# Rebuilding the first attention of a four-layer program: keys, queries and values through DRAM, transposed once, the diagonal masked on PE

## The reference, cut to what matters

```python
def _L1_xattn_ref(q, latent_kv, Wq, Wkv_expand, Wout):
    ...
    qp = q @ Wq.T
    kv = latent_kv @ Wkv_expand.T
    k, v = jnp.split(kv, 2, axis=-1)
    ...
    scores = jnp.einsum('bhqd,bhkd->bhqk', qh, kh) * inv_sqrt_d
    scores = jnp.where(causal, scores, jnp.finfo(scores.dtype).min)
    attn = jax.nn.softmax(scores, axis=-1)
    out = jnp.einsum('bhqk,bhkd->bhqd', attn, vh)
    ...
    return out @ Wout.T
```

## Time and profile before

| | us |
|---|---|
| median of 3 runs | 3899.13 (3897.04 to 3908.89) |
| the profiled execution | 3866.58 |
| its span | 3865.0 |
| busy: PE, DVE, ACT, POOL | 3227.9, 2331.7, 1878.8, 608.3 |
| mean granted clock of PE | 0.912 |

### The profile page before, as it was taken

One profiled execution on the slowest core, in us unless ns is written; L12 is line 12 of the kernel. 1 busy time (PEld: TensorE's weight loads), 2 busy tenths in 40 slices (PEclk: granted clock), 3 DMA queues, 4 the chain that ended last, 5 costly groups with the idle time before them and its releaser, 6 DMA issues. The chain is left out here.

```text
span 3865.0 us, 62264 instructions
## 1 busy us (share of the span) xinstructions
PE 3227.9 (84%) x16914; PEld 2254.7 (58%) x16918; DVE 2331.7 (60%) x3995; ACT 1878.8 (49%) x3267; POOL 608.3 (16%) x901
## 2 busy tenths in 40 slices
PE   4339996899985399956999789899899589979998
PEld 2127775666663288843333367788777333337886
DVE  6964445455535233347899545566556798965565
ACT  5643333255532155534777633466533477773343
POOL 2420000444420300021000130122111000010000
PEclk7669998999997599976999899999999699989999
DMA  4324444220001333334222252476644322212223
GB/s 145 137 99 137 138 138 130 104 82 0 0 12 54 111 109 103 109 114 153 53 52 53 80 184 93 154 245 238 209 137 128 119 53 52 57 31 80 95 94 115
DMA packets 191373, 405.52 MB, mean 105 GB/s; under 512 B 45893, under 2 KB 46021, under 8 KB 190579
## 3 DMA queue, kind: packets, MB, share of 16 engines
q1 hardware_dynamic: 157906, 287.52, 24.1%
q0 software_dynamic: 22480, 96.23, 7.3%
q10 hardware_dynamic: 10864, 20.45, 1.4%
HBM read 313.37 MB, written 88.08 MB: 104 GB/s over the span
## 5 line engine op out<-in xcount | busy, mean ns | idle before, releaser
L1646 DVE TENSOR_REDUCE at_maxima<-psum 128x1 f32<-128x512 f32 (+1 forms) x768 | 614.0, 861 | 53.8 <-PE psum L1547 52.0
L1625 ACT ACTIVATE at_probs<-psum 128x512 f32<-128x512 f32 x1024 | 528.8, 604 | 234.1 <-PE psum L1563 233.7
L1563 PE MATMUL psum<-at_qT,at_kT 50*128 50x512 f32 x1024 | 385.8, 458 | 90.4 <-ACT at_probs L1625 49.2
L573 PE MATMUL psum<-f_xT_hi,ffn_w_hi 128*128 x1024 | 407.8, 398 | 9.7 <-DVE f_xT_lo L313 2.2
L573 PE MATMUL psum<-f_xT_lo,ffn_w_hi 128*128 x1024 | 406.9, 397 | 0.0
L1563 PEld LDWEIGHTS psum<-at_qT,at_kT 50*128 50x128 f32 x1024 | 174.6, 191 | 385.2 <-ACT at_probs L1625 282.4
L1547 PE MATMUL psum<-at_kT,at_qT 48*128 48x512 f32 x1024 | 388.1, 481 | 9.6 <-DVE at_maxima L1646 7.7
L1576 PE MATMUL psum<-at_probs,at_vals 128*32 128x512 f32 x2048 | 282.4, 623 | 0.0
L590 PE MATMUL psum<-ffn_w_hi,ffn_hid_hi 128*128 128x512 f32 x768 | 269.3, 391 | 1.3 <-ACT ffn_hid_hi L636 1.3
L387 PE MATMUL psum<-ident,n_normed 128*128 128x128 f32 x448 | 94.7, 385 | 196.3 <-ACT n_normed L353 165.0
L478 ACT ACTIVATE ffn_w_hi<-ffn_w_raw 128x512 fp32r<-128x512 f32 x262 | 161.6, 633 | 158.8 <-PE psum L595 100.1
(11 more groups left out here) (396 smaller groups left out, 7245.5 us busy)
## 6 DMA issues: line engine op xcount, KB each, us to landing
ffn_w_raw<-in_stream SPq DMA_DIRECT2D x262, 256.0 KB, 2.8
ffn_w_hi<-quantized SPq DMA_DIRECT2D x66, 512.0 KB, 3.5
ffn_w_hi<-quantized SPq DMA_DIRECT2D x65, 256.0 KB
at_qT<-q_hi SPq DMA_DIRECT2D x256, 64.0 KB, 2.2
ffn2a_w_raw<-in_shared2a SPq DMA_DIRECT2D x26, 512.0 KB, 3.6
ffn2b_w_raw<-in_shared2b SPq DMA_DIRECT2D x26, 512.0 KB, 3.6
qz_raw<-in_stream SPq DMA_DIRECT2D x17, 768.0 KB, 4.2
quantized<-qz_quant POOLq DMA_DIRECT2D x16, 768.0 KB, 3.5
```

Of the source, the lines that this page charges most:

```text
L573: mm = pe.matmul(hid_ps[h][s][0:n, :], wt[s][:, w], xt[:, c, bass.ds(b * S, S)], start=(c == 0 and i == 0), stop=(c == DC - 1 and i == len ...
L1563: pe.matmul(scoreT[turn_of(n)][:, :], kT[r][half(h % 2, USED + 2), t * P:(t + 1) * P], qT[r][half(h % 2, USED + 2), h // 2, :], start=True ...
L1625: act.activation(probs[n % RING][:, :], scoreT[turn_of(n)][:, :], ACT.Exp, scale=factor).then_inc(exped, 1)
L1646: dve.tensor_reduce(maxima[:, h:h + banks, t], scores, AX.X, ALU.max).then_inc(maxed, 1)
```

## The change

The queries, keys and values of the first attention are made by a new stage and kept in DRAM. `stage_norm` makes x transposed, and its engines' orders are woven with the projections by hand. Queries and keys are multiplied with the features on the partitions, so no operand has to be turned later; each result is split (ACT hi, DVE lo) and stored, with the values padded to 64 columns a head (ones, then zeros). Per chunk that stores 512 KB of queries, 512 KB of keys and 512 KB of values.

The attention is then built like the second one: seven loads a group (three of queries, three of keys, 128 KB each, and 256 KB of values), the maxima out to DRAM and back by two puts. Groups run batch by batch. The values of a group lie in the ring of four that is loaded for group s+3, so the loads wait for the value products of s-1. Both masks stay products on PE, of the same size as before; POOL only makes the constants. `clear_slots` moves from SyncE to the head of ACT's order; SyncE waits for it at the end of the stage. `of_batch` (L2665) reads another layout with the same sizes. Constants of the new stage: RING = 8, SLOTS = 4, FIRST, LAST, MOVE, RES = 6, 3, 3, 6, TURNS = 3.

Of the diff, cut to its core (the old `stage_attend` and `stage_keys_values` are removed):

```diff
-def stage_norm(k, nm, xT=None, tokens=None, rows=None, joined=None, beside=None, before=None, bank=0):
+def stage_norm(k, nm, xT=None, tokens=None, rows=None, joined=None, beside=None, before=None, bank=0, woven=None):
...
-            with pe.Fori(0, B) as b:
+            def turn(b):
+
+            if woven is not None:
+                woven.pe(pe, turn, low, TB)
+                return
+            with pe.Fori(0, B) as b:
+                turn(b)
...
+def stage_causal_inputs(k, nm, weights_q, weights_kv, ctxT, q_parts, k_parts, c_parts, values):
...
+            def keep_kv(b, c):
+                i = DC * b + c
+                sp.wait_ge(k_hi, i + 1)
+                sp.wait_ge(k_lo, i + 1)
+                for dst, src in zip(k_parts, k_out[i % 2]):
+                    sp.dma_start(pieces(dst, c, b), src[:, :].bitcast(F32)).then_inc(k_kept[i % 2], DMA)
+                sp.wait_ge(v_made, i + 1)
+                sp.dma_start(values[i * P:(i + 1) * P, :], v_out[i % 2][:, :, :].rearrange("p h o -> p (h o)")).then_inc(v_kept[i % 2], DMA)
...
+            sp.dma_start(kv_raw[:, :], weights_kv).then_inc(kv_landed, DMA)
+            load_context(0)
+            load_context(1)
+            sp.dma_start(q_raw[:, :, :], weights_q).then_inc(q_landed, DMA)
+            keep_context(0)
+            sp.wait_ge(padded, 4)
+            for c in range(DC):
+                keep_kv(0, c)
+            keep_context(1)
+            for b in range(B):
+                for c in range(DC):
+                    keep_q(b, c)
+                    if b + 1 < B:
+                        keep_kv(b + 1, c)
+                if b + 2 < B:
+                    keep_context(b + 2)
...
+                def times_kv(b, c):
+                    i = DC * b + c
+                    if c == 0:
+                        pe.wait_ge(c_lo, b + 1)
+                    if i > 0:
+                        pe.wait_ge(k_hi, i)
+                        pe.wait_ge(k_lo, i)
+                    for m, (w, x) in enumerate(((0, 0), (0, 1), (1, 0))):
+                        mm = pe.matmul(kv_ps[0][:, :], wkv[w][:, c * P:(c + 1) * P], cT[b % 2][x][:, :], start=(m == 0), stop=(m == 2))
+                    mm.then_inc(k_product, 1)
+                    if i > 0:
+                        pe.wait_ge(v_made, i)
+                    for m, (w, x) in enumerate(((0, 0), (1, 0), (0, 1))):
+                        mm = pe.matmul(kv_ps[1][:, :], cT[b % 2][x][:, c * P:(c + 1) * P], wkv[w][:, D:2 * D], start=(m == 0), stop=(m == 2))
+                    mm.then_inc(v_product, 1)
+                def times_q(b, c):
+                    i = DC * b + c
+                    if c == 0:
+                        pe.wait_ge(x_made, x_before + TB * (b + 1))
+                    if i > 1:
+                        pe.wait_ge(q_hi, i - 1)
+                        pe.wait_ge(q_lo, i - 1)
+                    for kc in range(DC):
+                        for m, (w, x) in enumerate(((0, 0), (0, 1), (1, 0))):
+                            mm = pe.matmul(q_ps[i % 2][:, :], wq[w][:, kc, c * P:(c + 1) * P], xT[x][:, kc, b * S:(b + 1) * S],
+                                           start=(kc == 0 and m == 0), stop=(kc == DC - 1 and m == 2))
+                    mm.then_inc(q_product, 1)
+                pe.wait_ge(wkv_hi, 1)
+                pe.wait_ge(wkv_lo, 1)
+                for c in range(DC):
+                    times_kv(0, c)
+                turn(0)
+                turn(1)
+                pe.wait_ge(wq_hi, 1)
+                pe.wait_ge(wq_lo, 1)
+                for b in range(B):
+                    for c in range(DC):
+                        times_q(b, c)
+                        if b + 1 < B:
+                            times_kv(b + 1, c)
+                    if b + 2 < B:
+                        turn(b + 2)
...
+                act.wait_ge(kv_landed, DMA)
+                act.activation(wkv[0][:, :], kv_raw[:, :], ACT.Copy).then_inc(wkv_hi, 1)
+                part_context(0)
+                apply(0)
+                part_context(1)
+                act.wait_ge(q_landed, DMA)
+                act.activation(wq[0][:, :, :], q_raw[:, :, :], ACT.Copy).then_inc(wq_hi, 1)
+                for c in range(DC):
+                    take_kv(0, c)
+                move(0)
+                apply(1)
+                move(1)
+                apply(2)
+                for b in range(B):
+                    for c in range(DC):
+                        take_q(b, c)
+                        if b + 1 < B:
+                            take_kv(b + 1, c)
+                    if b + 2 < B:
+                        part_context(b + 2)
+                        move(b + 2)
+                    if b + 3 < B:
+                        apply(b + 3)
...
+                measure(0)
+                aggregate(0)
+                dve.wait_ge(wkv_hi, 1)
+                dve.tensor_tensor(wkv[1][:, :], kv_raw[:, :], wkv[0][:, :].bitcast(F32), ALU.subtract).then_inc(wkv_lo, 1)
+                part_context(0)
+                make_shift(0)
+                measure(1)
+                aggregate(1)
+                part_context(1)
+                dve.wait_ge(wq_hi, 1)
+                dve.tensor_tensor(wq[1][:, :, :], q_raw[:, :, :], wq[0][:, :, :].bitcast(F32), ALU.subtract).then_inc(wq_lo, 1)
+                for c in range(DC):
+                    take_k(0, c)
+                measure(2)
+                make_shift(1)
+                aggregate(2)
+                split(0)
+                measure(3)
+                split(1)
+                make_shift(2)
+                aggregate(3)
+                for b in range(B):
+                    for c in range(DC):
+                        take_q(b, c)
+                        if b + 1 < B:
+                            take_k(b + 1, c)
+                    if b == 0:
+                        make_shift(3)
+                    if b + 2 < B:
+                        part_context(b + 2)
+                        split(b + 2)
...
+def stage_attend_causal(k, nm, q_parts, k_parts, values, tops, y_g, factor, clear_slots, slots_cleared):
...
+        qT = [sb(f"qT{r}", [P, H, S], F32R) for r in range(SLOTS)]
+        kT = [sb(f"kT{r}", [P, H, S], F32R) for r in range(SLOTS)]
+        vals = [sb(f"vals{r}", [P, TB, H, OW]) for r in range(SLOTS)]
...
+        score, scoreT, res = room.banks[0:4], room.banks[4:4 + TURNS], room.banks[7]
...
+            def load(place, j):
+                b, n = batch_piece(place, j)
+                r, tokens = place % SLOTS, bass.ds(b * S, S)
+                for tile, (hi, lo), order in ((qT[r], q_parts, (0, 1, 0)), (kT[r], k_parts, (0, 0, 1))):
+                    for i, src in enumerate((hi, lo)[o] for o in order):
+                        rows = src[n * H * HD:(n + 1) * H * HD, tokens].rearrange("(h d) t -> d h t", h=H)
+                        sp.dma_start(tile[i * HD:(i + 1) * HD, :, :].bitcast(F32), rows).then_inc(landed[r], DMA)
+                rows = values[tokens, n * P:(n + 1) * P].rearrange("(t p) f -> p t f", p=P)
+                sp.dma_start(vals[r][:, :, :, :].rearrange("p t h o -> p t (h o)"), rows).then_inc(landed[r], DMA)
+            def send_max(place, g):
+                sp.wait_ge(max_turned, g + 1)
+                sp.dma_start(tops[place % SLOTS, :, :], across[place % 2][:, :]).then_inc(max_out, DMA)
+            def put_max(place, g):
+                r = place % SLOTS
+                sp.wait_ge(max_out, DMA * (g + 1))
+                rows = tops[r, :, :].rearrange("(b h o t) i -> h o t b i", b=TB, h=2 * H, o=2)
+                for h in range(H):
+                    dst = qT[r][USED:USED + 2, h, :].bitcast(F32).rearrange("o (t b i) -> o t b i", t=TB, b=TB)
+                    sp.dma_start(dst, rows[h]).then_inc(put[r], DMA)
+            sp.wait_ge(keys_cleared, SLOTS)
+            for g in range(SLOTS - 1):
+                load(g, 0)
+            send_max(0, 0)
+            put_max(0, 0)
+            def slot(s, place, j, ahead):
+                if ahead >= 1:
+                    send_max(place + 1, s + 1)
+                if ahead >= 3:
+                    if not is_first(s):
+                        sp.wait_ge(valued, RING + PAIRS * s)
+                    load(place + 3, j)
+                if ahead >= 1:
+                    put_max(place + 1, s + 1)
+            all_slots(sp, slot)
+            sp.wait_ge(slots_cleared, 3 * DMA)
...
+            def scores(g, place, j, n):
+                t, h = tile_head(n)
+                r, width = place % SLOTS, P * (t + 1)
                 if n == 0:
+                    pe.wait_ge(landed[r], LOADS * DMA * (use(place, j) + 1))
+                pe.wait_ge(maxed, PAIRS * g + n + 1)
+                pe.matmul(score[n % 4][:, 0:width], qT[r][0:USED, h, t * P:(t + 1) * P], kT[r][0:USED, h, 0:width], start=True, stop=True)
+                pe.matmul(score[n % 4][:, t * P:width], ident16[:, :], mask[:, :], start=False, stop=True,
```

(76 more changed lines are left out.)

595 lines of the change are left out of this document (179 added, 416 removed).

## The result

The kernel got slower: 3951.15 us in the median of 4 runs (3943.75 to 3953.86), against 3898.09 (3894.15 to 3908.89) for the kernel before on the same chip, a ratio of 1.0129 (95% interval 1.0104 to 1.0153), 53 us. The forecast was 32 us slower, 3931. Chips differ (the kernel before took 3863 to 3867 us beside the experiments), so kernels are compared by their ratio to it.

A forecast was written before the change was run, and what follows sets the result against it. The prediction took a chain (value products, seven loads, two puts) to bound each slot: 108 + 47 + 6.5 + 316.4 + 18.5 = 496.4 us against 464.0, 32.4 us slower, 3931 on the median; range 3885 to 3970.

The forecast's parts named there:

- Inputs: New stage making queries, keys and values: 108 us against 103.0 before, with ends of 90 and 120.
- The head: Attention stage's start to first exponential: 47 us, formerly 30.7; zeroing holds ACT 36.8 us, sharing DMA engines adds 10.5.
- The 25 without a hold: First exponential 25 us after the attention stage begins, if the zeroing does not hold ACT's queue.
- Slot 0: First group: 6.5 us, with two of its pairs done beforehand and half of the rest on the low clock.
- The 28 slots: Slot 1 to the start of slot 29: 9.9 + 0.3 + 1.15 = 11.3 us each, 316.4 us together.
- The clock in these slots: PE's loss to a lowered clock after standing on the puts: 1.15 us in each slot, between 0 and 1.7.
- two of my signs: New profile: PE idle some 2 us before most slots' first transposed score; granted clock near 0.85 through the stage.
- The last three slots: Slots from 29 on: 7.7 us without loads, then 5.4 each without scores of a later group, 18.5 together.
- the slot of 7.7 with PE as the bound: Attention slots: puts land before slot s ends, so a slot takes 7.7 us; kernel 3809 us, chance 0.05.
- neither hold nor clock would count: Head and slots: ACT not held, clock not falling, slot 10.0 us; sum 438, kernel 3873 us, chance 0.13.
- only one of the two would: Hold with slot 10.0: 460, kernel 3895 us; or no hold with slot 11.3: 474, kernel 3909; chance 0.17.
- The fourth rival: Stores bind the inputs (120 us) and slots take 12.5 us: sum 542, kernel 3977 us, chance 0.15.

The follow-up runs named there:

- e3: Changed kernel with the zeroing of the gather buffers issued by POOL, behind its constants, instead of by ACT: 1.0182 of the kernel before.
- e6: Changed kernel with the zeroing issued by POOL only after the eighth transposed score of slot 0: 1.0175 of the kernel before.
- e10: Changed kernel with e1's edit and the zeroing issued by POOL in the project stage, once its weights have landed: 0.9812 of the kernel before.
- e12: Changed kernel, all loads still behind the value products of s-1, but the values load moved just behind the puts: 1.0120 of the kernel before.
- e5: The changed kernel run again unchanged, on the same chip as three other experiments: 1.0161 of the kernel before.
- e1: Changed kernel with query and key loads waiting only for transposed scores of s-1, values load behind the puts: 0.9895 of the kernel before.
- e11: e10 with the three key loads of a slot issued by POOL at the slot's start, on their own semaphores: 0.9778 of the kernel before.
- e4: Changed kernel with nine unused 512-column products on PE ahead of the wait for the puts, in slots that load: 1.0156 of the kernel before.

## Why the prediction was right or wrong

The sign and the place were right, and so was the mechanism in the slots, a chain through SyncE's queue that makes PE stand and lose clock. The sum was too small, 496.4 against 528.9 us measured (645.4 to 1174.3; the 464.0 of before end 2.8 us ahead of the load by which the end is read here): 32 us slower was forecast, and the stages lost 61.9 in the first profile and 56.0 in the second. By its terms:

- Inputs: 108, measured 101.6 (645.4 to 747.0), so 1.4 less than before. The first query product starts 29.1 us into them where I had counted 33, the last one ends 67.7 later (I had 67), and the stage ends 4.8 after that (I had 4.5). So the 3 us for stores that bind were not needed, and the start was counted too long.
- The head: 47, measured 49.6 to the first exponential. The number was right and its reason half wrong. I made ACT's hold the cause and the crowd in the DMA engines an addition; e3 took the hold away (and made the store slower) and won nothing, e6 took the transfers away and won 24. The 25 without a hold came out as 24.8, but as the time without the transfers. In the kernel before no load or put had to pass the same zeroing; its list of DMAs from 748 to 790 us holds nothing else:

```profile
gathered<-zeros SPq DMA_DIRECT2D x1, 12288.0 KB
gathered<-zeros SPq DMA_DIRECT2D x1, 4096.0 KB
answers<-zeros SPq DMA_DIRECT2D x1, 2.0 KB
```

- Slot 0: 6.5, measured 11.5 (795.66 to 807.16). I had put half of it on the low clock; it ran there as a whole, behind 50 us in which PE had hardly worked. In e10, with a head half as long, it took 11.5 too.
- The 28 slots: 316.4, measured 338.7 (807.16 to 1145.81), 12.1 each where I had 11.3. In the parts, at full clock: PE up to the value products 3.9, measured 3.89; the loads 3.3, measured 3.39; the puts with their landing and the queue 2.95, measured 3.74. **This is the step that was mis-sized**, 0.8 us in 28 slots: I took the landing from the second attention, from a single row, and called its loads "such loads", though they are of 64 and 32 KB where these are of 128 KB, and none there is as large as the values load. For the values load I allowed 0.3, and e12 shows 0.5 to 0.7. The other 0.4 (e12's 3.07 against my 2.65) may be the larger loads; it was not tried.
- The clock in these slots: 1.15 a slot, measured 1.1. The 14 slots at full clock took 11.0 on the mean and the 14 at half clock 13.2 (10.8 and 13.4 in e5). The mean was luck. I had it as a loss in every slot, from one row, with 1.7 as the most that it could be; it is 2.2 in every second slot. So two of my signs were off: PE idles for over 3 us ahead of every second slot, not 2 us ahead of most, and the granted clock is 0.75, not near 0.85. It is most of a slot on half clock behind each stand of 3 us, and none, with one exception, behind those under 1 us. The Trainium skill (TensorE: Matmul & The Clock Gate, HAM oscillation) has every pass start on the halved clock; here it is every second one, since the cold slot is long enough to let the puts land and its own stand is short.
- The last three slots: 18.5, measured 28.5 to the end as read here. Slot 29 took 13.8 on the half clock; in e5 it fell on a slot at full clock and took 7.5. Another 2.8 us are the later end by which this term is read.

The differences are -6.4, +2.6, +5.0 (less 1.0, since PE starts ahead of ACT), +22.3 and +10.0: 32.5 us.

Of the rivals, the slot of 7.7 with PE as the bound was wrong for this kernel and right as its potential: the condition that I named, loads that wait only for the transposed scores, is e1's edit. It gave 8.79, though; 7.63 came only with POOL issuing the key loads (e11). That neither hold nor clock would count is refuted by ACT's 39.42 us and by the clock of 0.76, and with it that only one of the two would. The fourth rival's sum of 542 was nearer to the 528.9 than mine: its slot of 12.5 nearly came, by the landing more than by the clock, but its stores did not bind the inputs (101.6 us against its 120).

## What to carry to other kernels

Where work is moved off an engine into DMAs, count the chain through the issuing queue: every wait on it delays all that stands behind, and a small transfer that is needed soon must neither stand behind a wait for late work nor behind large loads. Put bulk transfers where nothing small has to pass them, here in a stage with a DMA share of 0.00; moving them to another engine's queue did not help (e3). A stand of PE costs more than its length when it brings the clock down, so filling it with useless products can pay in the stage; here the whole kernel did not measurably gain by that (e4), and taking the stand away did (e1, e11).

## What the runs showed that I had not expected

- A store of 16 KB took up to 19.2 us to be done beside the zeroing (e3), and 1.4 us (median, changed kernel) in the slots. While the engines were full, SyncE also needed mostly 1.2 to 1.6 us to issue a load where it needs 0.47 otherwise.
- The half clock came slot by slot: behind a stand of 3 us the next slot ran at 1.2 GHz, from its first product or from a later one (the fourth in the slot from 892.17), and behind one under 1 us the next ran at 2.4, with one exception. In between it was open: of e12's 18 stands of 1.6 to 2.8 us, 11 were followed by a slot at half clock.
- POOL issued two key loads in 1.07 us and one in 0.53, nearly as fast as SyncE, and they landed in time.
- The same kernel's stages behind the attention took 2765.4 and 2777.6 us in two executions with the same code, the longer one on the chip on which the kernel before took some 31 us more. Whether it is the chip is open; it wasn't tried.
